# Two of eight weighted copies in a mixture of experts, made on GpSimd in place of VectorE

## The reference

```python
x = x + jnp.tanh(g_xattn[0]) * attention0(ctx, _layernorm(x), ...)
x = x + jnp.tanh(g_ffn[0]) * mixture0(_layernorm(x), gate_w, We)      # the changed stage
...
def mixture0(x, gate_w, We):                    # gate_w [8, 128], We [8, 128, 128]
    logits = jnp.einsum('btd,ed->bte', x, gate_w)
    top_val, top_idx = jax.lax.top_k(logits, 2)
    top_w = jax.nn.softmax(top_val, axis=-1)
    y_all = jnp.einsum('btd,edm->btem', x, We)
    x_experts = jnp.take_along_axis(y_all, top_idx[..., None], axis=2)
    return jnp.sum(x_experts * top_w[..., None], axis=2)
```

## Time and profile before

| | |
|---|---|
| median of three runs | 2110.47 us (2106.33 to 2115.61) |
| the profiled execution's own time | 2107.25 us |
| its span | 2105.4 us |
| TensorE busy, matmuls / weight loads | 1896.9 us (90%) / 1449.0 us (69%) |
| VectorE busy | 1637.6 us (78%) |
| ScalarE busy | 1292.3 us (61%) |
| GpSimd busy | 371.8 us (18%) |
| line 876, the weighted copies | 128 of 0.683 us each, 631.2 to 768 us |
| granted clock of TensorE over the span | 0.951 |

### The profile page before, as it was taken

The page is one execution under the profiler, slowest core; times in us unless marked ns, Lnnn a source line. Parts: engine busy times, 40 slices in busy tenths (PEclk is TensorE's granted clock), DMA queues, the critical chain, the costliest instruction groups (busy, mean ns, idle before and its releaser), DMA issues. The chain is left out here.

```text
span 2105.4 us, 47401 instructions
## 1 busy us (share of the span) xinstructions
PE 1896.9 (90%) x17713; PEld 1449.0 (69%) x17713; DVE 1637.6 (78%) x4628; ACT 1292.3 (61%) x3167; POOL 371.8 (18%) x679
## 2 busy tenths in 40 slices
PE   7999999999969989999989897999999976899608
PEld 5787787877759988888867574677677765344208
DVE  5787887887859969999957796777777569787894
ACT  4777777777862318888856465455455267109744
POOL 1111111111111114433311142000000096000000
PEclk9999999999988999999989899999999999899859
DMA  5222221111116631111100022322232111002452
GB/s 151 59 67 55 52 59 47 44 45 44 46 53 242 242 132 33 34 34 33 30 1 1 11 60 69 109 83 83 85 120 85 52 41 31 0 0 120 182 177 81
DMA packets 123395, 152.32 MB, mean 72 GB/s; under 512 B 45817, under 2 KB 98594, under 8 KB 121122
## 3 DMA queue, kind: packets, MB, share of 16 engines
q1 hardware_dynamic: 119986, 147.71, 22.6%
q10 hardware_dynamic: 3184, 1.58, 0.3%
HBM read 110.19 MB, written 22.28 MB: 63 GB/s over the span
## 5 line engine op out<-in xcount | busy, mean ns | idle before, releaser
L1783 ACT ACTIVATE arena<-banks,b1c 128x512 f32<-128x512 f32 x192 | 131.5, 687 | 142.4 <-PE banks L1608 140.8
L1712 DVE TENSOR_TENSOR arena<-arena 128x512 f32<-128x512 f32 (+1 forms) x256 | 170.3, 686 | 57.5 <-ACT arena L1783 53.6
L623 ACT ACTIVATE arena<-banks,arena 128x128 f32<-128x128 f32 x512 | 180.1, 372 | 1.2 <-DVE arena L570 1.2
L499 PE MATMUL banks<-arena,wk 128*128 128x128 f32 x1024 | 134.8, 286 | 1.9 <-DVE arena L594 1.9
L1618 PEld LDWEIGHTS banks<-w2a,arena 128*128 128x128 f32 x1024 | 122.0, 192 | 20.1 <-issue 20.1
L499 PEld LDWEIGHTS banks<-arena,wk 128*128 128x128 f32 x1024 | 122.4, 196 | 13.3 <-issue 11.0
L538 PE MATMUL banks<-wv,arena 128*128 128x512 f32 x256 | 131.0, 594 | 0.0
L806 PE MATMUL banks<-we,arena 128*128 128x128 f32 x1024 | 127.5, 283 | 0.6 <-DVE arena L876 0.2
L1618 PE MATMUL banks<-w2a,arena 128*128 128x128 f32 x1024 | 124.7, 275 | 0.0
L806 PEld LDWEIGHTS banks<-we,arena 128*128 128x128 f32 x1024 | 121.3, 196 | 3.6 <-DVE arena L876 3.0
L1608 PE MATMUL banks<-arena,w1s 128*128 128x512 f32 x256 | 123.1, 615 | 0.0
(11 more groups left out here) (261 smaller groups left out, 5052.2 us busy)
## 6 DMA issues: line engine op xcount, KB each, us to landing
arena<-coef_scratch SPq DMA_DIRECT2D x32, 2048.0 KB, 8.3
arena<-arena SPq DMA_DIRECT2D x256, 64.0 KB, 2.0
gated_scratch<-arena SPq DMA_DIRECT2D x16, 768.0 KB, 3.2
arena<-gated_scratch SPq DMA_DIRECT2D x16, 768.0 KB, 4.3
arena<-z1T_scratch SPq DMA_DIRECT2D x128, 64.0 KB, 2.3
arena<-in_ctx_turned SPq DMA_DIRECT2D x32, 256.0 KB, 2.8
arena<-in_ctx SPq DMA_DIRECT2D x64, 64.0 KB, 2.1
z1T_scratch<-arena SPq DMA_DIRECT2D x64, 64.0 KB, 1.6
```

Source lines behind the costliest of these rows:

```text
L499: mm = pe.matmul(ps[:, n, c * P:(c + 1) * P], k.wk0[:, c * P:(c + 1) * P], Z[t.idx % 3][:, :, n], start=True, stop=True)
L623: act.activation(prob[:, o, c * P:(c + 1) * P], ps[:, SCORES + o, c * P:(c + 1) * P], ACT.Exp, bias=low[:, o, c:c + 1], accum_out=total[:, ...
L1712: dve.tensor_tensor(by_tile, by_tile, wide_coef[g.par][rows, e], ALU.mult).then_inc(s["scaled"].sem, 1)
L1783: act.activation(hT[g.par][:, c, :], ps[:, HID + c % NHID, :], ACT.Gelu, bias=k.b1c[:, c:c + 1])\
```

## The change

A constant `ON_DVE = 6` splits the eight copies. VectorE makes copies 0 to 5: three, the coefficient columns, three more. GpSimd makes copies 6 and 7 in each step, after its two small operations, with waits of its own for `xT`, for the spread coefficients and for the buffer (`out_psum` two groups back). They count up a semaphore of their own, `scaled_pool`. TensorE waits for it ahead of the seventh and the eighth expert of a group's first tile, SyncE ahead of the next spread transfer into the same buffer, and ScalarE ahead of the next `xT` in the same buffer. Thirteen lines are added, so the lines of VectorE's part move down by 12 (876 becomes 888).

```diff
--- before.py
+++ after.py
@@ -749,6 +749,7 @@
     ps, G = k.psum, k.T // GROUP
     f = group_signals(k, no)
     k.stage_memory()
+    ON_DVE = 6
     LIVE = 4
     xT = [k.take(GCOLS) for _ in range(LIVE)]
     xs = [v.rearrange("p (e n) -> p e n", e=EXPERTS) for v in (k.take(EXPERTS * GCOLS) for _ in range(2))]
@@ -764,7 +765,7 @@
     shift = k.take(GROUP)
     COLS = GROUP * EXPERTS
     XT, LOGITS, COEFT, OUT = 0, 1, 2, 3
-    s = k.sigs(G, dict(shift=1, l_psum=1, l_sb=1, gap=1, share=2, part=1, coef=1, ct_psum=1, ct_sb=1, scaled=EXPERTS,
+    s = k.sigs(G, dict(shift=1, l_psum=1, l_sb=1, gap=1, share=2, part=1, coef=1, ct_psum=1, ct_sb=1, scaled=ON_DVE, scaled_pool=EXPERTS - ON_DVE,
                        out_psum=1))
     coef_dram = k.nc.dram_tensor("coef0_scratch", [G, COLS, P], F32, kind="Internal").ap()
     coef_stored, coef_spread = k.transfers(G, "coef_stored"), k.transfers(G, "coef_spread")
@@ -783,6 +784,7 @@
                 sp.wait_ge(*coef_stored(g))
                 if g.has(2):
                     sp.wait_ge(*s["scaled"](g.back(2)))
+                    sp.wait_ge(*s["scaled_pool"](g.back(2)))
                 sp.dma_start(spread[g.par].rearrange("p e j n -> p j e n"),
                              coef_dram[g.idx].rearrange("(j e) n -> j e n", j=GROUP).partition_broadcast(P))\
                     .then_inc(coef_spread.at(g), 16)
@@ -794,6 +796,14 @@
                 if g.has(1):
                     pool.wait_ge(*f["xhat_ready"](sub(g.back(1), GROUP - 1)))
                 p_front(pool, g)
+            if g := at(1):
+                pool.wait_ge(*f["xT_sb"](g))
+                pool.wait_ge(*coef_spread(g))
+                if g.has(2):
+                    pool.wait_ge(*s["out_psum"](g.back(2)))
+                for n in range(ON_DVE, EXPERTS):
+                    pool.tensor_tensor(by_tile(xs[g.par][:, n]), by_tile(xT[g.idx % LIVE]), spread[g.par][:, n], ALU.mult)\
+                        .then_inc(s["scaled_pool"].sem, 1)
         yield from steps(pool, G, 4, 0, body)
 
     def tensor(pe):
@@ -801,8 +811,10 @@
             if j == 0 and g.has(2):
                 pe.wait_ge(*f["x_updated"](sub(g.back(2), GROUP - 1)))
             for n in range(EXPERTS):
-                if j == 0:
+                if j == 0 and n < ON_DVE:
                     pe.wait_ge(*s["scaled"](g, n + 1))
+                elif j == 0:
+                    pe.wait_ge(*s["scaled_pool"](g, n + 1 - ON_DVE))
                 mm = pe.matmul(ps[:, OUT + g.par, j * D:(j + 1) * D], xs[g.par][:, n, j * P:(j + 1) * P],
                                k.we0[:, n, :], start=n == 0, stop=n == EXPERTS - 1)
             if j == GROUP - 1:
@@ -898,7 +910,7 @@
             if far:
                 coefficients(far)
             if nxt:
-                weigh(nxt, 3, EXPERTS)
+                weigh(nxt, 3, ON_DVE)
         yield from steps(dve, G, 4, 1, body)
 
     def scalar(act):
@@ -930,6 +942,7 @@
                 act.wait_ge(*f["xT_psum"](g))
                 if g.has(LIVE):
                     act.wait_ge(*s["scaled"](g.back(LIVE)))
+                    act.wait_ge(*s["scaled_pool"](g.back(LIVE)))
                 act.activation(xT[g.idx % LIVE], ps[:, XT, :], ACT.Copy).then_inc(f["xT_sb"].sem, 1)
         yield from steps(act, G, 4, 0, body)
 
```

## The result

The changed kernel is slower by 0.31%: the ratio of its times to those of the kernel before is 1.0031, with a 95% interval of 1.0021 to 1.0042. In microseconds that is +6.5 (+4.4 to +8.9); the medians of 20 runs each are 2117.43 and 2109.85, which lie 7.6 apart. Its profiled execution took 2111.64 us with a span of 2109.8, at the low end of its runs, as that of before was.

What follows compares the result with a forecast made beforehand. VectorE's chain was taken to bound the step at 8.87 us, TensorE just behind. +0.27 us a step x 11 plus 0.8 at the ends gave +3.8 us: 2114 us against the median, range 2105 to 2122.

Steps and rivals of the forecast that it cites:

- A: The forecast itself: GpSimd copies hold VectorE 1.01 us in turns, VectorE stays the bound, 2114 us; chance 0.50.
- C: Rival: the hold lasts GpSimd's whole record and line 687's cast stands too; +0.98 us a step, 2123 us; chance 0.13.
- What is removed: VectorE's copies in each step: two of eight go, at 0.60 us each, saving 1.20 us.
- TensorE's floor of 8.65: Each step: TensorE could do it in 8.65 us, the least that unloading VectorE can reach from 8.87.
- GpSimd's copies of 1.26 us: GpSimd, behind its root of line 725: two copies of 1.26 us, inputs ready, new waits on TensorE cost nothing.
- The hold of 1.01: VectorE operation beside a GpSimd copy: can't begin its work until 1.01 us after the copy's start.
- First hold 0.46: GpSimd's first copy in a step: VectorE's line 691 stands 0.46 us.
- The second hold: GpSimd's second copy in a step: line 866 or the first VectorE copy stands 1.01 us.
- Turns: GpSimd and VectorE alternate, so each GpSimd copy can hold VectorE once at most, whichever asks first.
- B: Rival: GpSimd gives way earlier for two-input operations, hold 0.78 or less, step is TensorE's; 2108 to 2109 us; chance 0.32.
- D: Rival: GpSimd's copies lose their turns and reach TensorE late; 2121 us at 1 us late; chance 0.03.
- Ends: Ends of the stage: first two steps cost 0, the last two groups together +0.8 us.

Runs made afterwards that it cites:

- the hidden copy and the old order: Changed kernel with one copy on GpSimd, started when VectorE is at its last copy, TensorE's order unchanged; step 9.14 us, stage 169.8 us, one run.
- The memset kernel: Changed kernel with GpSimd's two copies replaced by four memsets that only write, experts 6 and 7 left out; step 8.62 us, ratio 0.9984.
- an order for TensorE alone: Kernel before, all copies on VectorE; TensorE takes coefficient transposes and logits first, xhat's transposes amid the fourth tile's outputs; step 8.87 us, ratio 0.9977.

## Why the prediction was right, and by how much it was short

The forecast was A: 2114, slower by 3.8 us, with VectorE held in turns and still the bound. Measured: +6.5 us (4.4 to 8.9), 2117.4, inside the range and a change of under 0.5%, to which the largest chance was given. The mechanism was right, the forecast a good half of the size. The step's growth of +0.60 lies halfway between A's +0.27 and C's +0.98, so A is the better description because of what happened (holds in turns, each over before the record's end), not because of the number.

- *What is removed, 1.20 us a step, TensorE's floor of 8.65.* Right: 8.62 and 8.59 in the kernels where no hold sets the step.
- *GpSimd's copies of 1.26 us behind line 725, inputs there, no wait of TensorE for them.* Right: 1.27, and no such wait.
- *The hold of 1.01.* This term was sized too small. Measured from GpSimd's start it is 709.20 - 708.07 = 1.13 for the first copy and 710.42 - 709.30 = 1.12 for the second, which started at 709.30.
- *First hold 0.46, on line 691.* This term is off by more. The hold fell on the cast of line 687, which I had counted among what rival C brings, and where nothing comes late ahead of the cast it is 0.78. The second hold, 1.02 for 1.01, fell on line 691 and not on the bias or a copy. So 1.47 a step should have been 1.80, and +0.27 was +0.60; the step measured 9.47, not 9.14. Of the 0.32 by which the first hold was short, 0.11 is the length of the hold and 0.21 is the cast, which stands that much earlier in the row than line 691.
- *Turns, each GpSimd copy holds once.* Right, in the steady part and among copies.
- *Rivals.* B fell, since a two-input operation was held like the others. C's second half was true (the cast), its first was not: VectorE began 0.14 us ahead of the copy's recorded end, and the step was 9.47, not 9.85. D fell.
- *The logits.* I had no term for it. With VectorE's last copy two experts earlier, TensorE has three experts to load before the logits, and line 856 comes 0.18 later. In the steady part that cost nothing, since the chain through GpSimd is longer; at the ends it is likely a good part of what was missed, for with copies 0 and 1 on GpSimd the stage is 1.9 us shorter there. With the hidden copy and the old order the loop through the logits cost more than the copy gained (9.14 against 8.87).
- *Ends.* I took all of steps 1 to 11 for steps of 8.87; step 1 was 10.21, with a wait of 1.23 us for the logits in it, and didn't grow. At the start +0.9 where I gave 0, beside a wait for the logits of 2.26 in place of 1.41, and in the last groups +2.0 for +0.8, both as read from one pair of profiles. 5.84 us for the last group's copies against 5.7 was right; that its spread transfer is issued later, behind a longer step of TensorE, was missing.

The sum by the measured terms is 0.60 x 10 steps (step 1 was no longer than before), less 0.1, and 2.9 at the ends: 8.8 in the stage. The timed difference is 6.5, and its interval ends at 8.9.

The page SBUF — State Buffer of the Trainium skill, section "Who interferes with whom", also says that a cast can contend while a two-input operation contends only with reads. The memset kernel shows exactly that pair: the cast held by up to 0.41 us, line 691 not at all.

## What to carry to other kernels

Before work is moved from VectorE to GpSimd, list what VectorE does while GpSimd would read: each operation with two SBUF inputs, each cast, and each operation like line 199's that meets a GpSimd copy stands until about 0.15 us before the copy's end (0.25 in the earlier trace rows). At up to 1.13 us held (here 0.78 and 1.02) for 0.60 us saved, the move loses where VectorE is the bound. It was free beside statistics (0.87 us as ever), beside the searches of line 685 (0.16), and beside operations with an input in PSUM: in the trace of the kernel before, 55 operations of line 1111 ran beside GpSimd's 128x512 operations, none over 0.26 us. When two engines are nearly equal bounds, look also at the order of the engine that follows: here an order for TensorE alone gave 4.9 us (2.1 to 7.6), of which the stage shows 2.7.

## What the runs showed of the hardware that was not expected

- A GpSimd operation that only writes (memset, 0.53 us) held a VectorE cast of 8 columns by up to 0.41 us, while an operation with two SBUF inputs ran beside it at full speed.
- Time that VectorE stands held is recorded as the operation's own duration: line 691 shows 1.31 us for 0.29 of work, and VectorE's busy share of 95% (90.31 of 95 us) hid it.
- A GpSimd copy that began 0.25 us into the second of three VectorE copies read only behind the third, and was recorded as 2.30 us for 1.27. The root in the earlier trace rows began 0.07 us into the first of three copies and had its turn behind that one. Why the turn came one copy later there is open.
